# Attention of the first layer: masked queries and transposed weights, or heads in row groups with the scores computed twice

## The reference

```python
Q = (x @ W_Q.T).reshape(b, s, H, HD).transpose(0, 2, 1, 3)      # H = 16 heads of HD = 8
attn = jnp.einsum('bhqd,bhkd->bhqk', Q, K) / jnp.sqrt(jnp.float32(HD))
slopes = 1.0 / (2.0 ** 8) ** ((jnp.arange(H, dtype=jnp.float32) + 1) / H)
rel = jnp.minimum(pos[None, :] - pos[:, None], 0).astype(jnp.float32)
bias = slopes[:, None, None] * rel[None, :, :]
attn = jnp.where(causal[None, None], attn + bias[None], -jnp.inf)
attn = jax.nn.softmax(attn, axis=-1)
out = jnp.einsum('bhqk,bhkd->bhqd', attn, V)
return out.transpose(0, 2, 1, 3).reshape(b, s, d) @ W_O.T
```

## Time and profile before

| | us |
|---|---|
| median of 3 runs | 1691.79 |
| lowest, highest | 1689.09, 1692.54 |
| the profiled execution: its time | 1694.99 |
| its span, first to last instruction | 1693.2 |
| instructions | 34235 |
| busy of the span: PE 1281.7, DVE 951.2, ACT 592.8, POOL 263.8 | |

### The profile page before, as it was taken

One profiled execution on the slowest core, in us unless ns is written; L12 is line 12 of the kernel. 1 busy time (PEld: TensorE's weight loads), 2 busy tenths in 40 slices (PEclk: granted clock), 3 DMA queues, 4 the chain that ended last, 5 costly groups with the idle time before them and its releaser, 6 DMA issues. The chain is left out here.

```text
span 1693.2 us, 34235 instructions
## 1 busy us (share of the span) xinstructions
PE 1281.7 (76%) x11002; PEld 965.0 (57%) x11002; DVE 951.2 (56%) x3327; ACT 592.8 (35%) x1531; POOL 263.8 (16%) x280
## 2 busy tenths in 40 slices
PE   6999998999988113533699777699817897979782
PEld 4999996566645113510466452355405897979772
DVE  3666665344423776656645668444586265656423
ACT  3555552222220201132122121133311375757562
POOL 3322210000000000000000000222020343434332
PEclk9999998999999565666799878699957598989896
DMA  6996000000000000000172001333180121212111
GB/s 246 367 357 242 0 0 1 29 19 19 10 1 1 1 1 2 2 0 0 43 152 51 6 1 41 89 103 100 34 278 1 53 58 37 59 35 58 43 42 55
DMA packets 93077, 111.58 MB, mean 66 GB/s; under 512 B 13888, under 2 KB 66071, under 8 KB 92304
## 3 DMA queue, kind: packets, MB, share of 16 engines
q1 hardware_dynamic: 85200, 100.87, 19.7%
q0 software_dynamic: 7760, 9.25, 1.8%
HBM read 61.14 MB, written 53.43 MB: 68 GB/s over the span
## 5 line engine op out<-in xcount | busy, mean ns | idle before, releaser
L1654 PE MATMUL m_psY<-large,m_hT 128*128 x992 | 142.4, 288 | 4.8 <-issue 2.5
L1640 PE MATMUL m_psH<-m_xT,m_up 128*128 128x128 f32 x992 | 139.7, 286 | 0.0
L1654 PEld LDWEIGHTS m_psY<-large,m_hT 128*128 128x128 f32 x992 | 129.8, 195 | 5.6 <-issue 5.5
L1640 PEld LDWEIGHTS m_psH<-m_xT,m_up 128*128 128x128 f32 x992 | 129.3, 203 | 0.1
L1580 POOL DMA_INDIRECT rows<-m_ys,m_slot x93 | 90.4, 972 | 132.2 <-DVE m_slot L1848 117.3
L815 DVE SCALAR_TENSOR_TENSOR m_hid<-m_psU,m_wu,m_sg 128x512 f32<-128x512 f32 x64 | 48.1, 751 | 92.2 <-ACT m_sg L802 92.2
L1299 PE MATMUL m_acc<-se_place,se_parts 128*128 128x512 bf16 x384 | 89.5, 384 | 0.0
L1697 ACT ACTIVATE m_up<-large 128x512 f32 x124 | 78.1, 630 | 28.6 <-DVE m_valid L1751 17.2
L802 ACT ACTIVATE m_sg<-m_psG,m_wu 128x512 f32<-128x512 f32 x64 | 44.0, 687 | 123.3 <-PE m_psU L764 123.3
L424 ACT ACTIVATE at_Pr<-at_S,at_nmax 128x128 f32<-128x128 f32 x128 | 51.4, 402 | 98.8 <-DVE at_nmax L380 98.6
L776 PEld LDWEIGHTS m_psD<-m_wd,m_hid 128*128 128x128 f32 x512 | 67.0, 191 | 31.3 <-issue 30.4
(11 more groups left out here) (537 smaller groups left out, 2898.5 us busy)
## 6 DMA issues: line engine op xcount, KB each, us to landing
rows<-blank SPq DMA_DIRECT2D x2, 19584.0 KB, 103.2
m_xs<-rows SPq DMA_DIRECT2D x124, 76.5 KB
large<-in_L_attn_firs SPq DMA_DIRECT2D x4, 2048.0 KB, 16.6
large<-comb_rows SPq DMA_DIRECT2D x64, 128.0 KB, 5.2
se_wu<-in_L_ffn_up SPq DMA_DIRECT2D x32, 192.0 KB
W2T<-in_L_ffn_down_turned SPq DMA_DIRECT2D x1, 4096.0 KB, 12.5
large<-in_L_ffn_up SPq DMA_DIRECT2D x4, 1024.0 KB, 8.1
large<-in_L_ffn_down SPq DMA_DIRECT2D x16, 256.0 KB, 6.9
```

Of the source, the lines that this page charges most:

```text
L1640: m = nc.tensor.matmul(psH[b][:, c * P:(c + 1) * P], up[b][:, c * P:(c + 1) * P], xT[b][:], start=True, stop=True)
L1654: m = nc.tensor.matmul(psY[b][:, 0:wide], hT[b][:, c * P:(c + 1) * P], k.W2[:, bass.ds(e + c * WIDE, wide)], start=(c == 0), stop=(c == C ...
```

## The change

K and Q move to a layout in which a head owns 32 partitions. KA and QA are 128 rows by 4 groups by 2048 tokens; head 4g + i sits in rows 32i of group g: 8 rows of features, one row that carries slope times key position in KA against a one in QA, one row that carries the negated peak of the query in QA against a one in KA. The other 22 rows are filled: ones in KA, zeros in QA. A product then contracts over 32 rows and bias and peak come out of it.

The scores are computed twice. First with the queries on partitions (`scores`, as before but K = 32 rows), after a bfloat16 product of the identity with the causal mask (`hide_later`) over the two diagonal blocks; DVE takes the maximum of each row and block from PSUM (one tensor_reduce of 384 columns). Per sequence the peaks are turned, negated and copied out by ACT, and four DMAs put them into QA (`send_peaks`). Then with the keys on partitions (`dots`): ACT takes the exponential of 384 columns straight from PSUM to PT, with the slope's share as bias, and POOL sets the future entries of the two diagonal blocks to zero (`affine_select`). `weigh` takes four heads at a time: V, widened to 32 columns a head with a column for the sum (VA), is the weights, PT moves, and head i's result goes to partitions 32i. So a sequence's result has features on partitions; it is copied out (`raw`), turned back by four transposes and divided by its sums.

A step of the order on PE has two heads of scores and two of dots that lie 26 heads (`LEAD`) behind, in four different row groups, so: two `hide_later`, four products of 256 columns, four of 128; every second step one `weigh`. The masking of queries, the table of biases, S, the transposes of Pr and their copies are gone.

Q and K rows reach QA and KA by DMA: the first two sequences by 4 DMAs a group for Q and 4 for K, the rest in a second part of 16 and 16. SP sends Q, the first group's K and the small rows (28 DMAs before the last group is complete), ACT the K rows of three groups (12), POOL the K rows of the second part (16).

The setup loads the four weights, fills KA (8192 columns a partition, DVE), VA (8192, POOL) and QA (POOL one quarter, ACT three), and PE makes five products with a blank operand before the transposes. `start_delta_loads` comes after the peaks of two sequences and no longer holds the filters: these are loaded at the end of the first experts' queue on SP (`start_fir_loads`), since KA and VA lie in the large buffer. `clear_rows` moves to the first block of the delta scan. W_O's rows are laid out in the new order of heads on the host.

```diff
-def setup_stage(k, x_in):
+def setup_stage(k, a):
...
+    for w, n in ((k.at_wq, "Q"), (k.at_wk, "K"), (k.at_wv, "V"), (k.at_wo, "O")):
+        sp.dma_start(w, a[f"L0_attn_W_{n}"]).then_inc(k.tally("at_w_in").sem, 16)
+    sp.wait_ge(*sloped.at(1))
+    sp.dma_start(k.at_slope[:], k.at_row[:].rearrange("p (i g) -> p i g", i=4)).then_inc(k.tally("x_in5").sem, 16)
...
+    nc.gpsimd.memset(k.at_QA[:, 3, :], 0.0).then_inc(made.sem, 1)
+    pool.wait_ge(*made.at(9))
...
+    dve.drain()
...
+    for i in range(WARMING - 3):
+        nc.tensor.matmul(idle[:], k.ident[:], k.blank[:, 0:512], start=True, stop=True)
     pe.wait_ge(*loaded.at(16))
     for g in range(4):
         for j in range(4):
             t = nc.tensor.transpose(ps[:, g, j * P:(j + 1) * P], k.X[:, 4 * g + j, :], k.ident[:])
...
+    act.wait_ge(*blank.at(1))
+    for g in range(3):
+        nc.scalar.activation(k.at_QA[:, g, :].rearrange("p (x n) -> p x n", n=512),
+                             k.blank[:, 0:512].unsqueeze(1).to_broadcast([P, 4, 512]), ACT.Copy)
     for g in range(4):
...
-def attention_stage(k, a, w_q, w_k, w_v, w_o):
+def attention_stage(k, a):
...
+    LEAD = 26
+    PRING, TRING = 12, 3
+    ALL = BATCH * HEADS
...
+        def few_rows(g):
+            sp.dma_start(KA[HD:P:32, g, :].rearrange("i (b n) -> i b n", n=SEQ),
+                         k.at_slopes[:, g, :].unsqueeze(1).to_broadcast([TILES, BATCH, SEQ])).then_inc(rows_in[g].sem, 16)
+            sp.dma_start(QA[HD:P:32, g, :], KA[HD + 2:HD + 6, g, :]).then_inc(rows_in[g].sem, 16)
+        few_rows(0)
+        for g in range(GROUPS):
+            sp.wait_ge(*q_out.at(1))
+            for i in range(TILES):
+                rows, head = head_rows(g, i)
+                sp.dma_start(QA[rows, g, 0:512], QT[head, 0:512]).then_inc(rows_in[g].sem, 16)
+            if g == 0:
+                sp.wait_ge(*k_out.at(1))
+                for i in range(TILES):
+                    rows, head = head_rows(g, i)
+                    sp.dma_start(KA[rows, g, 0:512], KT[head, 0:512]).then_inc(rows_in[g].sem, 16)
+            if g + 1 < GROUPS:
+                few_rows(g + 1)
+        def send_peaks(b):
+            sp.wait_ge(*peak_out.at(b + 1))
+            for g in range(GROUPS):
+                sp.dma_start(QA[9:P:32, g, b * SEQ:(b + 1) * SEQ], peakT[4 * g:4 * g + 4, b % 2, :])    .then_inc(peak_in[b % 2].sem, 16)
+        sp.wait_ge(*q_out.at(4))
+        for g in range(GROUPS):
+            for i in range(TILES):
+                rows, head = head_rows(g, i)
+                sp.dma_start(QA[rows, g, 512:N], QT[head, 512:N]).then_inc(more_rows_in[g].sem, 16)
+            if g == 0:
+                send_peaks(0)
+        send_peaks(1)
         start_delta_loads(k, a, sp)
+        for b in range(2, BATCH):
+            send_peaks(b)
     @block.gpsimd
     def _(pool):
...
+        pool.wait_ge(*k_out.at(4))
+        for g in range(GROUPS):
+            for i in range(TILES):
+                rows, head = head_rows(g, i)
+                nc.gpsimd.dma_start(KA[rows, g, 512:N], KT[head, 512:N]).then_inc(more_keys_in.sem, 16)
+        pool.wait_ge(*cleared.at(2))
+        pool.wait_ge(*v_out.at(8))
+        nc.gpsimd.tensor_tensor(VA[:, :, :, 0:18], VA[:, :, :, 0:18],
+                                k.at_weight[:].unsqueeze(1).unsqueeze(3).to_broadcast([P, T, HEADS, 18]),
+                                ALU.mult).then_inc(cleared.sem, 1)
+        pool.wait_ge(*cleared.at(3))
+        for v in range(ALL):
+            pool.wait_ge(*expd.at(v + 1))
+            nc.gpsimd.affine_select(out=diag(PT[:, v % PRING]), in_=diag(PT[:, v % PRING]), compare_op=ALU.is_ge,
+                                    fill=0.0, base=0, pattern=[[0, 2], [1, P]], channel_multiplier=-1)\
+                .then_inc(cleared.sem, 1)
...
+        def hide_later(u):
+            if u >= TILES:
+                pe.wait_ge(*reduced.at(u - TILES + 1))
+            out = psS[:, u % TILES, 0:CAUSAL].rearrange("p (x c) -> p x c", c=P)
+            nc.tensor.matmul(diag(out), identb[:], maskb[:].unsqueeze(1).to_broadcast([P, 2, P]),
+                             start=True, stop=False, skip_group_check=True)
+        def scores(u, part):
+            b, g, r = operands(u)
+            rows = slice(r, r + 32)
+            if part == 0:
+                return nc.tensor.matmul(psS[:, u % TILES, P:CAUSAL], QA[rows, g, keys(b, 1)],
+                                        KA[rows, g, b * SEQ:(b + 1) * SEQ],
+                                        start=False, stop=True, skip_group_check=True)
+            return nc.tensor.matmul(psS[:, u % TILES, 0:P], QA[rows, g, keys(b, 0)], KA[rows, g, keys(b, 0)],
+                                    start=False, stop=True, skip_group_check=True).then_inc(scored.sem, 1)
+        def dots(v, part):
+            b, g, r = operands(v)
+            rows = slice(r, r + 32)
+            if part == 0:
+                return nc.tensor.matmul(psT[:, v % TRING, 0:SEQ], KA[rows, g, keys(b, 0)],
+                                        QA[rows, g, b * SEQ:(b + 1) * SEQ], start=True, stop=True,
+                                        skip_group_check=True)
+            return nc.tensor.matmul(psT[:, v % TRING, SEQ:CAUSAL], KA[rows, g, keys(b, 1)],
+                                    QA[rows, g, keys(b, 1)], start=True, stop=True,
+                                    skip_group_check=True).then_inc(dotted.sem, 1)
...
+        def weigh(q):
+            b, quad = divmod(q, GROUPS)
+            for kt in range(2):
+                for i in range(TILES):
+                    h, slot = TILES * quad + i, (TILES * q + i) % PRING
+                    o = psO[32 * i:32 * i + 32, half + kt * P:half + SEQ]
+                    x = PT[:, slot, 2 * kt:2 + kt, :].rearrange("p x c -> p (x c)")
+                    m = nc.tensor.matmul(o, VA[:, 2 * b + kt, h, :], x, start=quad % 2 == 0 and kt == 0,
+                                         stop=quad % 2 == 1 and kt == 1, skip_group_check=True)
+            m.then_inc(weighted.sem, 1)
...
+        for step in range(-LEAD // 2, ALL // 2 + 4):
+            us = [u for u in (2 * step + LEAD, 2 * step + LEAD + 1) if 0 <= u < ALL]
+            vs = [v for v in (2 * step, 2 * step + 1) if 0 <= v < ALL]
+            for u in us:
...
+                    pe.wait_ge(*more_rows_in[u // TILES - 2 * GROUPS].at(64))
...
+                if v == 0:
+                    pe.wait_ge(*v_out.at(8))
+                if v >= TRING:
+                    pe.wait_ge(*expd.at(v - TRING + 1))
+            for part in range(2):
+                for u in us:
+                    scores(u, part)
+                for v in vs:
+                    dots(v, part)
+            done = 2 * step + 2
+            if done == HEADS + TILES - LEAD:
+                turn_peaks(0)
+            if done >= 2 * TILES and done % TILES == 0 and done // TILES - 2 < QUADS:
+                q = done // TILES - 2
+                weigh(q)
+                if q % GROUPS == 0 and q // GROUPS + 1 < BATCH:
+                    turn_peaks(q // GROUPS + 1)
+            if done % HEADS == 6 and HEADS < done:
+                turn_raw(done // HEADS - 1)
...
+        act.wait_ge(*k_out.at(1))
+        for g in range(1, GROUPS):
+            for i in range(TILES):
+                rows, head = head_rows(g, i)
+                act.dma_start(KA[rows, g, 0:512], KT[head, 0:512]).then_inc(rows_in[g].sem, 16)
...
+        def copy_peaks(b):
+            act.wait_ge(*turned.at(b + 1))
+            if b >= 2:
+                act.wait_ge(*peak_in[b % 2].at(64 * (b // 2)))
+            nc.scalar.activation(peakT[:, b % 2, :], psO[0:HEADS, SEQ:2 * SEQ], ACT.Copy).then_inc(peak_out.sem, 1)
+        for v in range(ALL):
+            act.wait_ge(*dotted.at(v + 1))
+            if v >= PRING:
+                act.wait_ge(*weighted.at((v - PRING) // TILES + 1))
+            nc.scalar.activation(PT[:, v % PRING, :, :].rearrange("p x c -> p (x c)"),
+                                 psT[:, v % TRING, 0:CAUSAL], ACT.Exp,
+                                 bias=k.at_bias[:, v % HEADS:v % HEADS + 1]).then_inc(expd.sem, 1)
+            b, n = divmod(v, HEADS)
+            if n == 2 * TILES - 1 and b + 1 < BATCH:
+                copy_peaks(b + 1)
+            ended = b - 1 if n == TILES - 1 else (b if v == ALL - 1 else -1)
+            if ended >= 0:
+                act.wait_ge(*weighted.at(GROUPS * (ended + 1)))
+                nc.scalar.activation(raw[:, ended % 2, :], psO[:], ACT.Copy).then_inc(raw_out.sem, 1)
...
+        for u in range(ALL):
+            b, n = divmod(u, HEADS)
+            dve.wait_ge(*scored.at(u + 1))
+            nc.vector.tensor_reduce(peaks[:, b % 2, n, :],
+                                    psS[:, u % TILES, 0:CAUSAL].rearrange("p (x c) -> p x c", c=P),
+                                    AX.X, ALU.max).then_inc(reduced.sem, 1)
+            if n == HEADS - 1:
...
```

(11 more changed lines are left out.)

356 lines of the change are left out of this document (175 added, 181 removed).

## The result

The changed kernel takes 1644.3 us (median of 4 runs, 1637.27 to 1649.9) where the kernel before took 1692.16 in the same session: ratio 0.9716 [0.9668, 0.9764]. It is faster by 48 us; the forecast was 97. The profiled execution has a span of 1647.0 us instead of 1693.2.

A forecast was written before the change was run, and what follows sets the result against it. PE bounds the attention loop at 1.65 us a head. New loop end 38.5 + 107.5 + 10 + 4 = 160 against 257.0, gaining 97 us: 1598 profiled, 1595 median. Range 1562 to 1650.

The forecast's parts named there:

- What bounds the kernel, and where the gain is: Attention loop: PE sets 1.65 us a head; the gain comes from its 226 us stretch, 30.97 to 257.00.
- Do row groups overlap: New loop on PE: products in four row groups overlap fully, 0.66 us a step; bounds 0.66 and 2.64.
- rival 2: Attention loop: weight loads don't hide (27 us) or layout changes drain (21 us); 1616 to 1643 us; chance 0.23.
- The chain, "can't be shorter than 1.47": Attention loop: products, results out, exponential and semaphores take 1.47 us a step without `weigh`; with it 1.89.
- Ahead of the loop ... dots start at 38.5: Before the attention loop: row issues 0.47 us apart, landing 2.0, scores at 0.52 a head; dots start at 38.5.
- Rival 4, the clock falls: Attention loop: waits lower PE's clock to 0.5, doubling products, 79 us: 1674 us; chance 0.07.
- Moved DMAs ... Cost nothing: Clearing moved from attention to the scan's first block: gains nothing, costs nothing; at most some 10 us without cover.
- The prediction's own sign of being wrong: A head costs under 0.65 or over 1.1 us, or a stage behind attention changes by more than 3 us.
- Setup: Block before attention: ends at about 13.5 us; products start at 13.8, at full clock if blank products raise it.
- The sum: Whole kernel: attention loop ends at 160 instead of 257.0, gain 97 us, profiled execution 1598, median 1595.

The follow-up runs named there:

- e8: Changed kernel with clearing moved to the delta filters' block, K's second part sent after the first lands, and exponential over 192 of 384 columns: 1616.65 us, ratio 0.9559.
- e3: Changed kernel, with POOL sending the second part of K only after multiplying V and after the first part has landed: 1626.17 us, ratio 0.9709.
- e5: Changed kernel, with the products of scores and dots contracting over 10 rows instead of 32: 1704.38 us, ratio 1.008.
- e2: Kernel before, with only its clearing moved from beside attention to the scan's first block: 1697.27 us, ratio 1.013.
- e9: Changed kernel with clearing in the delta filters' block, K's second part sent after the first lands, and no blank products in the setup: 1621.73 us, ratio 0.9578.
- after: The changed kernel itself, with the whole change against the kernel before: 1644.3 us, ratio 0.9716.
- e1: Changed kernel, with the two clearing DMAs issued in the block of the delta filters instead of the scan's first block: 1615.13 us, ratio 0.9653.

## Why the prediction was wrong, step by step

- **What bounds the kernel, and where the gain is**: right. Attention gave nearly all of the gain. (One reading was loose: the first of the six slices stands at 6 tenths, not at 9.)
- **Do row groups overlap**: right, starts 0.02 us apart. The size was off: products 0.86 a step, not 0.66. The 3.07x of the Trainium skill ("TensorE: Matmul & The Clock Gate", section on packing small matmuls) gave 0.86 and was closer than my extrapolation from the 32x32 row; that it fits to the hundredth is partly chance, since its case is one round of 512 columns and here are two rounds, of 256 and 128. Of rival 2 some 0.2 us a step is there, 13 us in all and not its 27 and 21. That 1644 lies next to its 1616 to 1643 is a coincidence: the time was lost elsewhere.
- **The chain, "can't be shorter than 1.47"**: the mechanism was right (e8), the terms too small: products 0.20 more, exponential 0.04, the hops between engines the rest of 0.29. The 0.1 for two semaphores stood on no row. Steps 1.76 and 1.98 instead of 1.47 and 1.89. With 32 of each kind (9.3 + 2.9), plus 4.4 for the first five steps at half clock, less 6 on the changes of sequence (1.0 instead of 1.3 extra us each, 7 not 8 of them) and on the last 26 heads, which have dots only (1.66 a step): the 64 steps took 128.1 us instead of 117.5. With the end, dots to W_O took 133.3 instead of 121.5: +12.
- **"Ahead of the loop ... dots start at 38.5"**: this term failed, +23 us. Issues were priced at 0.47 from rows of one plain 64 KB load each by one queue; these cost 0.67 alone and up to 1.05 beside two other issuing queues. Landings were priced at 2.0 from the same loads; the third group's took 10.4 with POOL's 16 larger DMAs under way, and 1.4 for the last group without them (e3). Steps of two scores were priced by DVE's 0.52 a head; PE needs 1.18 a step even at full clock, and 2.12 at half clock. Estimated shares of the 23 us: nine such steps after 40.93, with the turning of the peaks, lose some 9 to the clock. In e3 the last rows come at 35.09 instead of 29.7, so some 5 are the issues. The 8 to 9 left are the landings. The prediction looked for POOL's DMAs holding up POOL, and not for what they do to the rows of the other two queues.
- **Rival 4, the clock falls**: I asked the question for the loop, where the filled rows answer it (e5), and not for the stretch ahead of it, where it did fall. Some 13 us (9 + 4.4) in all; the 4.4 was 2 us less in the executions where the clock came back a step earlier.
- **"Moved DMAs ... Cost nothing"**: failed, +21.5 us. I asked who waits for SP and for the data, and nobody did; I didn't ask who else uses the DMA engines. The scan has DMA share 0.01 and looked free, but its small products use up code fast (16 KB packets at 586.33 and 589.80), and their fetches go through the same engines. The prediction's own sign of being wrong, a stage behind attention that changes by more than 3 us, came true here. That attention wouldn't gain from losing the clearing was right (e2).
- **Setup**: the block ended at 12.4 instead of 13.5, better than forecast, and the blank products gained nothing (e9).
- **The sum**: 23.0 + 11.8 + 1.0 (W_O's product and after, now partly at half clock) = 35.8 on attention, 21.5 on delta, 5.8 and 0.7 gained elsewhere: 50.8, which is 1648.8 of the profiled execution against 1598. The 5.8 us in the later stages have no cause here, and some 3 of them are scatter: in the second trace of the changed kernel these stages are 2.5 us shorter than before. By that trace the excess is 30.4 on attention and 20.7 on delta.

## What to carry to other kernels

Before a large transfer is moved to a stretch "where the DMA engines are free", look for pauses marked "issue" in dense runs of small instructions there: code comes by the same engines, and full engines turn short stops into long ones. Price the issue of a DMA by a row of its own shape, with as many queues issuing as there will be, and its landing with the transfers that will be under way beside it. Price the stretch ahead of the loop at the clock that it will be granted, step by step, as carefully as the loop. Rows of ones against zeros that fill up the contraction can be worth more than they cost: here 60 us, all of it the clock.

## What the runs showed of the hardware

- Four products in four row groups: starts within 0.02 us, and 0.86 us for a round of 256 columns and one of 128. The sets overlap; 0.11 us at the start, most likely the first weight load, and 0.11 at the end do not.
- The granted clock followed the number of rows contracted: 10 rows instead of 32 gave 0.57 in a loop that had 1.00 (e5), though PE was busy 57.2 of 60 us against 52.0.
- A small SBUF to SBUF DMA (8 rows of 2 KB) holds its queue 0.67 us on SP, 0.79 to 0.99 on ACT beside others, 0.53 on POOL. It landed 1.4 us behind its issue (e3), and 10.4 us behind it with 16 DMAs of 48 KB from POOL under way (after).
- 39 MB of writes in flight lengthened pauses in the scan's products (1.1 to 4.9 us at the one shown) and the stage by 21 us (e1, e2). The six pauses that grew end 1.2 to 1.6 us behind the end of a 16 KB code packet, with and without the writes; with them the packet moved later.
